# First routing cut into portions behind VectorE's bias additions, prefix sums moved to the end of batch 0

## What is computed

```
xn = layernorm(x)
scores = Q K^T / sqrt(8) + rel_bias          # 16 heads, 256 x 256 for each sequence
s = softmax(scores) V Wo + bo
probs = softmax(xn @ gate_W)                 # 8 experts
topk_w, topk_idx = top_k(probs, 2)           # weights divided by their sum
g = silu(layernorm(0.5 gelu(xn @ shared_W) + sum over the 2 chosen experts e of w_e * ffn_e(xn)))
x = x + s * g
```

## Time and profile before

| | us |
|---|---|
| median of three runs | 840.21 |
| lowest, highest run | 838.3, 841.58 |
| span of the profiled execution | 871.4 |
| busy in it: TensorE | 720.9 |
| VectorE | 572.6 |
| ScalarE | 488.3 |
| GpSimd | 453.8 |

### The profile page before, as it was taken

How to read it: one execution, slowest core, us unless ns; L and a number is a source line. 1 busy time by engine, 2 the same in 40 slices (tenths; PEclk the granted TensorE clock), 3 DMA queues, 4 the chain that set the end, 5 groups by cost and what they waited for, 6 DMA issues and landing times. The chain is left out here.

```text
span 871.4 us, 16890 instructions
## 1 busy us (share of the span) xinstructions
PE 720.9 (83%) x5338; PEld 491.0 (56%) x5338; DVE 572.6 (66%) x1292; ACT 488.3 (56%) x919; POOL 453.8 (52%) x398
## 2 busy tenths in 40 slices
PE   2776786879899999979999889899977557999890
PEld 2651131223333333338889878799866456999780
DVE  7778888888888899943334276656374665454345
ACT  1663564558787888865454538568721135455460
POOL 7912343458888999982454444400025743455451
PEclk9998698789999999989999999999977789999995
DMA  8995351013222323135888886440001421677956
GB/s 246 357 270 185 117 160 49 26 55 100 73 88 70 101 74 93 53 117 166 238 251 243 258 257 214 148 125 1 1 13 40 131 75 37 198 217 219 285 158 187
DMA packets 115377, 124.09 MB, mean 142 GB/s; under 512 B 10608, under 2 KB 97312, under 8 KB 115328
## 3 DMA queue, kind: packets, MB, share of 16 engines
q1 hardware_dynamic: 107200, 106.71, 41.5%
q0 software_dynamic: 8128, 16.78, 5.4%
HBM read 82.50 MB, written 40.81 MB: 142 GB/s over the span
## 5 line engine op out<-in xcount | busy, mean ns | idle before, releaser
L696 POOL DMA_INDIRECT yg_dram<-work x138 | 136.1, 986 | 163.9 <-DVE work L1771 139.8
L1275 ACT ACTIVATE work<-wide,work 128x256 f32<-128x256 f32 x324 | 131.6, 473 | 114.4 <-PE wide L913 111.6
L1426 DVE TENSOR_REDUCE work<-wide 128x4 bf16<-128x1024 f32 x128 | 156.9, 1227 | 31.2 <-PE wide L791 25.0
L924 PE MATMUL wide<-work 128*128 128x128 f32 x1296 | 159.2, 277 | 0.0
L924 PEld LDWEIGHTS wide<-work 128*128 128x128 f32 x1296 | 153.2, 193 | 0.6
L913 PE MATMUL wide<-xT,work 128*128 128x256 f32 x552 | 135.3, 389 | 9.7 <-issue 8.3
L913 PEld LDWEIGHTS wide<-xT,work 128*128 128x128 f32 x552 | 101.8, 195 | 24.6 <-issue 12.3
L659 POOL TENSOR_TENSOR work<-work,biasT 128x1024 f32<-128x1024 f32 x32 | 75.8, 2368 | 68.1 <-ACT work L1213 67.3
L659 POOL TENSOR_TENSOR yy<-yy,biasT 128x1024 f32<-128x1024 f32 x32 | 75.7, 2366 | 34.5 <-ACT yy L1213 34.1
L1220 ACT ACTIVATE yy<-yy 128x1024 f32<-128x1024 f32 x64 | 67.5, 1055 | 42.0 <-DVE yy L1673 33.7
L816 PE MATMUL wide<-work 49*128 49x256 bf16 x512 | 53.1, 288 | 41.7 <-DVE yy L1673 16.8
(11 more groups left out here) (288 smaller groups left out, 1226.3 us busy)
## 6 DMA issues: line engine op xcount, KB each, us to landing
work<-in_wcat SPq DMA_DIRECT2D x73, 578.0 KB
work<-stk_dram SPq DMA_DIRECT2D x128, 96.0 KB
xg_dram<-empty SPq DMA_DIRECT2D x35, 260.0 KB, 2.6
work<-xg_dram SPq DMA_DIRECT2D x69, 130.0 KB
stk_dram<-yy SPq DMA_DIRECT2D x16, 384.0 KB, 3.4
stk_dram<-yy SPq DMA_DIRECT2D x16, 256.0 KB, 3.2
yy<-yg_dram SPq DMA_DIRECT2D x8, 512.0 KB, 6.5
biasT<-ext_dram SPq DMA_DIRECT2D x1, 3072.0 KB
```

The lines of the kernel that those rows point to most:

```text
L696: g.indirect_dma_start(out=yg_dram[l], out_offset=bass.IndirectOffsetOnAxis(ap=yid[v][:, s_:s_ + 1].bitcast(u32), axis=0), in_=yb[u][:, s_ ...
L924: last = mm(YP[u][:, s_ * D:(s_ + 1) * D], hb[u][:, c, s_ * P:(s_ + 1) * P], wb[v][:, HID + c * D:HID + (c + 1) * D], start=(c == 0), stop ...
L1275: A(hb[u][:, c, :], bank[2 + 2 * u + c // 2][:, (c % 2) * TS:(c % 2 + 1) * TS], ACT.Gelu, bias=wb[v][:, bc:bc + 1]).then_inc(m["gelu"], 1)
L1426: V.tensor_reduce(nmax[:, :, 2 * place(t):2 * place(t) + 2].rearrange("p c e -> p e c"), into[:, :].rearrange("p (e c k) -> p e c k", e=2, ...
```

## The change

The blocks are split into smaller functions and called at other places. In batches 0 to 3 each odd step calls `route_first_layer` directly behind `add_bias` and ahead of `reduce_maxima`. `route_keep_counts` moves from step 7 of batch 1 to step 0 of batch 1, `route_pe` from step 7 of batch 1 to step 7 of batch 0, where it waits for the first copied maxima of batch 1. The wait for `kept` moves from `project_out` to the second transposes of maxima of batch 1. No instruction of the routing is added or dropped, and the order of its steps differs only in that the weights (`route_weights`) come behind the tile counts. For the second layer the helpers are called in the former order.

```diff
@@ transpose_maxima
                 elif g == 0 and n == 1 or g == 1:
                     pe.wait_ge(a["nmT"], n * 2 + g)
+                    if n * g:
+                        pe.wait_ge(rou[0]["kept"], 1)
@@ project_out
                 pe.wait_ge(a["onT"], b + 1)
-                pe.wait_ge(rou[0]["kept"], 1)
@@ attend
-                    if t == 7 and back == 1:
-                        pe.wait_ge(a["onT"], 1)
+                    if t == 7 and back == 0:
+                        pe.wait_ge(a["nmT"], 3)
                         route_pe(0, E0, PX[:, 0:T * E0], PX[:, T * E0:2 * T * E0])
...
-            def route_choose(l, k):
+            def route_rest(l):
+                logit, e1 = lg[:, :, 0:(E0, E1)[l]], by_token(rt[1], l)
+                st.link(V.scalar_tensor_tensor(e1, by_token(hot[0], l), OFF, logit, ALU.mult, ALU.add))
+                st.link(V.reduce_max((pk[1] if l == 0 else tmpa)[:, :], e1, AX.X))
+
+            def route_match(l, k):
...
+                st.link(V.tensor_tensor(e2, among, over(top[:, :], ne), ALU.is_equal))
+                st.link(V.tensor_tensor(e2, e2, mid(eidx[:, E0 - ne:E0], T), ALU.mult))
+
+            def route_first(l, k):
...
                 st.link(V.tensor_reduce(tmpb[:, :], e2, AX.X, ALU.min))
-                st.link(V.tensor_tensor(hotk, eb, over(tmpb[:, :], ne), ALU.is_equal))
+                st.link(V.tensor_tensor(hotk, mid(eidx[:, E0 - ne:E0], T), over(tmpb[:, :], ne), ALU.is_equal))
...
-            def route_weights(l):
+            def route_chosen(l):
                 n = T * (E0, E1)[l]
                 V.tensor_tensor(rt[3][:, 0:n], hot[0][:, 0:n], hot[1][:, 0:n], ALU.add).then_inc(rou[l]["A"], 1)
+
+            def route_weights(l):
...
-            def route_tiles(l):
-                ne = (E0, E1)[l]
-                n = (T - FIRST[l]) * ne
+            def route_sums(l):
+                n = (T - FIRST[l]) * (E0, E1)[l]
                 st.link(V.memset(rt[2][:, 0:n], 1.0))
                 st.link(V.tensor_tensor_scan(rt[0][:, 0:n], rt[2][:, 0:n], rt[1][:, 0:n], 0.0, ALU.mult, ALU.add))
                 st.link(V.tensor_tensor(rt[1][:, 0:n], rt[0][:, 0:n], rt[1][:, 0:n], ALU.subtract))
+
+            def route_tiles(l):
+                ne = (E0, E1)[l]
...
+            def route_first_layer(b, t):
+                if b == 0:
+                    if t == 1:
+                        route_match(0, 0)
+                        route_first(0, 0)
+                    elif t == 3:
+                        route_rest(0)
+                        route_match(0, 1)
+                    elif t == 5:
+                        route_first(0, 1)
+                        route_chosen(0)
+                elif b == 1:
+                    if t == 1:
+                        route_sums(0)
+                    elif t == 3:
+                        route_tiles(0)
+                    elif t == 5:
+                        route_weights(0)
+                    else:
+                        route_half_counts()
+                elif b == 2:
+                    if t == 1:
+                        route_halves()
+                    elif t == 3:
+                        route_sides()
+                    elif t == 5:
+                        route_places()
+                    else:
+                        route_slots(0, (0,))
+                elif t == 1:
+                    route_slots(0, (1,))
+                elif t == 3:
+                    route_tile_ends(0)
+                elif t == 5:
+                    route_late_ends()
+                else:
+                    route_rows(0)
+
             def attend_dve(b, back=2, ahead=True, part=None):
                 for t in range(NPAIR):
                     if t % 2:
                         add_bias(b, t)
+                        if part is not None:
+                            route_first_layer(part, t)
                     if ahead:
                         reduce_maxima(b + 1, t)
-                    if part == 0 and t == 3:
-                        route_choose(0, 0)
...
-                    elif part == 1 and t == 7:
+                    if part == 1 and t == 0:
                         route_keep_counts(0, bank[7][:, 0:T * E0], bank[7][:, T * E0:2 * T * E0])
```

More of the change, by code:

```diff
@@ L1493, in route_probabilities @@
                 st.link(V.tensor_tensor(e0, e0, over(tmpb[:, :], ne), ALU.mult))
-            def route_choose(l, k):
-                ne = (E0, E1)[l]
[L1497 to L1500, removed]
-                hotk = by_token(hot[k], l)
[L1502 to L1507, removed]
+            def route_rest(l):
[3 more added lines that the diff above has]
+            def route_match(l, k):
+                ne = (E0, E1)[l]
+                among = by_token(rt[1], l) if k else lg[:, :, 0:ne]
+                e2 = by_token(rt[2], l)
+                top = pk[k] if l == 0 else tmpa
+                st.link(V.tensor_tensor(e2, among, over(top[:, :], ne), ALU.is_equal))
+                st.link(V.tensor_tensor(e2, e2, mid(eidx[:, E0 - ne:E0], T), ALU.mult))
+            def route_first(l, k):
+                ne = (E0, E1)[l]
+                e0, e2 = by_token(rt[0], l), by_token(rt[2], l)
+                hotk = by_token(hot[k], l)
                 st.link(V.tensor_reduce(tmpb[:, :], e2, AX.X, ALU.min))
-                st.link(V.tensor_tensor(hotk, eb, over(tmpb[:, :], ne), ALU.is_equal))
+                st.link(V.tensor_tensor(hotk, mid(eidx[:, E0 - ne:E0], T), over(tmpb[:, :], ne), ALU.is_equal))
                 if l:
@@ L1554, in route_tiles, with route_half_counts @@
                 st.link(V.tensor_scalar(ecnti[:, 0:hi], ecnti[:, 0:hi], TS.bit_length() - 1, None, ALU.logical_shift_right))
+            def route_half_counts():
+                ne = E0
+                early, late = slice(0, ne), slice(ne, 2 * ne)
+                cnt, tend = ecnt[0:2]
+                st.did(V.tensor_copy(cnt[:, early], ecnti[:, late]))
+                st.link(V.tensor_tensor(cnt[:, late], ecnti[:, early], ecnti[:, late], ALU.subtract))
+                st.link(V.tensor_tensor_scan(tend[:, :], rt[2][:, 0:2 * ne], cnt[:, :], 0.0, ALU.mult, ALU.add))
             def route_halves():
@@ L1574, in route_places @@
                 st.link(V.tensor_tensor(e0, e2, mid(elim[:, 0:E0], T), ALU.is_lt))
+            def route_places():
+                e0, e2 = routed_rows(rt[0], 0), routed_rows(rt[2], 0)
                 st.link(V.tensor_tensor(e2, e2, mid(ecnt[3][:, E0:2 * E0], T), ALU.add))
@@ L1611, in route_places_second, with route_slots @@
                 st.link(V.tensor_tensor(e2, e2, e0, ALU.add))
-            def route_slots(l):
+            def route_slots(l, choices=range(TOPK)):
                 e0, e2 = routed_rows(rt[0], l), routed_rows(rt[2], l)
-                for k in range(TOPK):
+                for k in choices:
                     st.link(V.tensor_tensor(e0, e2, by_token(hot[k], l)[:, FIRST[l]:T, :], ALU.mult))
@@ L1622, in route_slots, with route_tile_ends, route_late_ends @@
                         st.did(ins)
+            def route_tile_ends(l):
+                ne, nj = (E0, E1)[l], (NJ0, NJ1)[l]
+                wide_ = ne if l == 0 else NPART * ne
+                ej = ejm[:, 0:nj * wide_].rearrange("p (j e) -> p j e", e=wide_)
+                st.link(V.tensor_tensor(ej, mid(ecnt[1][:, 0:wide_], nj), over(jidx[:, 0:nj], wide_), ALU.is_le))
+                st.link(V.reduce_sum(ejf[:, 0:nj], ej, AX.X))
+            def route_late_ends():
+                ej = ejm[:, 0:NJ0 * E0].rearrange("p (j e) -> p j e", e=E0)
+                st.link(V.tensor_tensor(ej, mid(ecnt[1][:, E0:2 * E0], NJ0), over(jidx[:, 0:NJ0], E0), ALU.is_le))
+                st.link(V.reduce_sum(ejg[:, 0:NJ0], ej, AX.X))
+                st.link(V.tensor_tensor(ejf[:, 0:NJ0], ejf[:, 0:NJ0], ejg[:, 0:NJ0], ALU.add))
             def route_rows(l):
@@ L1937, in _ @@
             for k in range(TOPK):
-                route_choose(1, k)
+                if k:
+                    route_rest(1)
+                route_match(1, k)
+                route_first(1, k)
+            route_chosen(1)
             route_weights(1)
             route_keep_counts(1, bank[0], bank[1])
+            route_sums(1)
             route_tiles(1)
```

29 lines of the change are left out of this document (3 added, 26 removed).

## The result

The changed kernel takes 815.13 us (median of 5 runs, 811.98 to 816.87), the kernel before 840.21 us. The ratio is 0.971, with a 95% interval from 0.968 to 0.974: 25.1 us less, where 19.9 were forecast. The median lies just inside the lower end of the forecast's range, 815 to 829.5.

What follows compares the result with a forecast made beforehand. VectorE was taken as the bound: base 59.6, routing 17.5, GpSimd waits 1.0, prefix sums 1.1, other idle 2 give 81.2 us for four batches instead of 101.1; 840.2 - 19.9 = 820.3 us, range 815 to 829.5.

Steps and rivals of the forecast that it cites:

- Waits for GpSimd: Routing steps on VectorE in batches 0 to 3 wait for GpSimd's bias additions: 11.8 us before, 1.0 us after.
- The side that spoke against the change: A portion beyond 2.1 us would delay GpSimd's addition up to 0.43 us; 6 us of GpSimd, 0 of the kernel.
- The prefix sums: Moved to the end of batch 0, they occupy TensorE and leave VectorE idle 1.1 us.
- The wait for their copies: Moved to the transposes of batch 1's second half of maxima; TensorE may stand 0.5 us, cost to the kernel 0.
- Other idle time: VectorE's remaining idle time in batches 0 to 3, mostly at the end of batch 0: 2 us, bounds 0 and 8.8.
- the base of 59.6 us without routing: VectorE's occupied time in the first four batches without the routing: 88.9 - 29.3 = 59.6 us.
- The floor: Lower end for the first four batches, nothing idle and no wait: 77.1 us, kernel 816.2 us.
- batches 5 to 8 at 17.4: Sign that the forecast is right: these batches without routing stay at 17.4 us each, as before.
- A: Rival: portions still meet GpSimd's additions, each waiting 0.7 us; four batches 90.2 us, kernel 829.3; chance 0.27 together with B.
- B: Rival: VectorE's idle time of bare batches stays; four batches 88 us, kernel 827; chance 0.27 together with A.
- C: Rival: TensorE granted 1.2 GHz through all four batches becomes the bound; about 107 us, kernel 846; chance 0.04.
- D: Rival: no effect, the gain is lost further on, as in the scatter's start; kernel 840; chance 0.04.

Runs made afterwards that it cites:

- e7: Changed kernel with one more linked two-input step of 256 elements behind each of the 16 odd bias additions of batches 0 to 3: four batches 85.2 us, ratio 0.985.
- e3: Changed kernel with each portion behind the reduction of its odd step instead of ahead of it: four batches 84.1 us, ratio to before 0.981.
- e5: Changed kernel with the routing in six undivided blocks behind odd bias additions instead of 15 portions: four batches 101.8 us, ratio to before 0.999.
- e4: Changed kernel with every portion one step earlier, ahead of the odd pair's bias addition, where the blocks stood before: four batches 104.4 us, ratio to before 1.006.
- e1: Kernel before with GpSimd's bias additions of batches 0 to 3 cut to 8 of 256 columns: four batches 85.8 us, ratio to before 0.986.

## Why the prediction was right

**The bound.** VectorE was to be the bound without slack. It is busy 74.7 of 77.2 us, and e7 adds its work in full.

**Waits for GpSimd.** 11.8 us were read off eight steps, 1.0 forecast to stay. In the changed kernel the three rows above, L1506, L1587 and L1569, exceed their own lengths (0.42, 0.60, 0.15) by 0.2, 0.2 and 0.3, together 0.8. The prediction took the own length of L1587, before's L1573, as 0.43: its waits were 11.6 and the routing's own work 17.7. The 2.1 us between a bias addition and GpSimd's start, read from one pair of batch 5, is what e3 and e5 turn on: it is 2.08 or 2.09 us at 14 of the 16 additions that start in these batches, 2.16 and 2.26 at the others. Short portions directly behind the bias addition gain; the same portions 1.1 us later lose 6.9 us, in the even steps 27, and long blocks in the right place about 24. Here the trace bears out what the Trainium skill, "SBUF — State Buffer", section "Who interferes with whom", says: whichever of the two comes first holds the shared ports for its whole instruction and the other waits. e3 shows VectorE waiting 2.07 us; e7 shows GpSimd's addition 0.17 us longer where 0.30 us of VectorE's step were left. The side that spoke against the change costs what the prediction said, nothing.

**The prefix sums.** 1.1 us of idle time forecast, 0.88 in the row at 100.46. The wait for their copies ahead of the transposes holds TensorE 0.6 us once, 0.5 forecast, and VectorE has no gap there, as forecast.

**The size.** 81.2 us forecast for the four batches, 77.2 measured; the saving was put at 19.9 and is 23.9 by the same first profile. Two terms of the sum were too large. "Other idle time", taken as 2 us, is nearly nothing: VectorE's only gap of over 0.1 us in these batches is that of the prefix sums, where the first profile of before has 20. And the base of 59.6 us without routing comes out at 77.2 - 17.7 - 0.8 - 0.9 = 57.8. Its instructions are as long as before; what shrank is that they follow each other without a gap, and then each starts some 0.1 us before the last has ended: two reductions in a row take 2.36 us, one alone 1.22 or 1.23. The floor that I gave as an end, 77.1, is where it landed, but partly by luck: that sum has neither a wait nor the prefix sums in it, and the smaller base pays for both. What is left of the 25.1 us can't be placed so finely: between the two profiled executions, 840.6 and 809.9 us, 24.3 us lie in the four batches, 1.7 in batch 4 (16.48 and 18.20), and 3.7 behind the attention, a time that differs by 6 us among the profiles of the shorter kind. The sign "batches 5 to 8 at 17.4" failed by the chip alone.

**The rivals.** A, portions that still meet GpSimd: not in the change, and exactly what e4 is. B, bare idle time that stays: no. C, the clock: it is 1.00 in batches 1 to 3, against 0.85, 0.85 and 0.74; in batch 0 0.83. D, a gain lost further on: no, but batch 9 shows how it could be. The argument against D, that GpSimd's queue waits only for VectorE's results and ScalarE's copies, was wrong there. In before GpSimd's wait for its scatters there goes with 19.81 - 16.48 = 3.3 us on the shorter chip too, so it is no part of the difference.

**What the prediction had wrong in its reasons.** It treated the waits for GpSimd and TensorE's stalls as two sums that the change removes one by one, and so I expected division or place alone to bring a part (e5). They don't: a long block in either place meets an addition and stalls TensorE, and a short one in the old place meets it every time. From 101.4 to 76.9 us, 15.6 us go when GpSimd's additions are small and nothing else is changed (e1), and 8.9 more with division and place; but with the additions whole neither half of the edit brings anything. A small slip: the blocks have four to ten steps, not eleven.

## What to carry to other kernels

Work added to the bound engine should be cut to fit between the event that releases the next engine and the start of the neighbour that shares its ports: measure that window in the trace (2.1 us here) before choosing the piece. Division and place have to be right together; an experiment with either alone would have said that it is useless. And when a step of known size takes several times its length in one spot, look for what another engine ends at that moment.

## What was not expected of the hardware

Tiny steps with a single SBUF tensor as input wait for GpSimd just as two-input ones do: in e4 a TENSOR_SCALAR of 32 elements took 1.57 us and a CAST of 8 elements 1.97. A TENSOR_REDUCE does not: L1513 ran its 0.41 us from 96.50 on, in the midst of the addition of 95.12, and the two-input step behind it waited for the addition's end. The prediction's mechanism spoke of two-input steps and one cast. That a portion of reductions alone could stand anywhere would follow, but was not tried.

The same program differs by 31 us between chips while the single instructions agree: in batches 6 to 8 of the two profiles of before, matmuls, reductions and additions have the same mean duration (0.384 us for the 512-column matmul in both). Batches without routing take 16.48 us on one and about 17.4 on the others, and the 52 indirect transfers of the second layer's scatter, from the first issue to the last, 67.6 us against 82.5. What sets this is open.
